# A router's mean taken in four groups of tiles, and the last output tiles in two pairs

## Reference

```python
xn = _layernorm(x)
x  = x + gnn(xn, edges) + mix(xn)              # x1: what the edge batches make
x2 = _layernorm(x)
logits = mean(x2, axis=nodes) @ Wr + br        # one row of 8
w = softmax(scale * softmax(logits)); top 2    # two experts, two weights
y = sum over the 2 experts: w_e * (gelu(x2 @ W1_e + b1_e) @ W2_e + b2_e)
x = x + layernorm(y + x2) * gamma + beta
```

## Time and profile before

| | us |
|---|---|
| median of 3 runs | 2583.76 (2582.44 to 2586.27) |
| the profiled execution | 2590.89 |
| its span | 2589.1 |
| busy: PE, DVE, ACT, POOL | 1962.0, 1677.4, 954.5, 1576.9 |
| mean granted TensorE clock in it | 0.867 of full speed |

### The profile page before, as it was taken

One profiled execution on the slowest core, in us unless ns is written; L12 is line 12 of the kernel. 1 busy time (PEld: TensorE's weight loads), 2 busy tenths in 40 slices (PEclk: granted clock), 3 DMA queues, 4 the chain that ended last, 5 costly groups with the idle time before them and its releaser, 6 DMA issues.

```text
span 2589.1 us, 32776 instructions
## 1 busy us (share of the span) xinstructions
PE 1962.0 (76%) x8612; PEld 1426.1 (55%) x8612; DVE 1677.4 (65%) x3588; ACT 954.5 (37%) x2092; POOL 1576.9 (61%) x1713
## 2 busy tenths in 40 slices
PE   5667787767776776867767678888787666899997
PEld 4545555545555554545555556666565443577775
DVE  6567676767767676666766677777778885333334
ACT  2533333333333343333333432323224554433332
POOL 2477777777777777777777777777777772000000
PEclk9878878888888888888888888888898778899998
DMA  7455555555555555555555556556555551100000
GB/s 234 153 157 147 148 146 147 149 147 147 148 148 146 148 146 145 153 140 148 148 145 146 141 158 172 163 165 167 165 163 144 135 138 40 39 19 18 18 18 20
DMA packets 171510, 337.61 MB, mean 130 GB/s; under 512 B 36500, under 2 KB 89466, under 8 KB 171342
## 3 DMA queue, kind: packets, MB, share of 16 engines
q0 software_dynamic: 78144, 220.11, 31.4%
q1 hardware_dynamic: 91854, 115.32, 15.4%
q10 hardware_dynamic: 1344, 0.27, 0.1%
HBM read 309.16 MB, written 26.39 MB: 130 GB/s over the span
## 4 chain that ended last, share of the span: by engine, by line
POOL 33%; PE 20%; issue 20%; DVE 11%; DMA 8%; POOLq 4%; ACT 3%; DVEq 2%; ACTq 0%; SPq 0%
POOL work L662 33%; DMA work<-h_tab,cols 7%; PE bank L1146 6%; PE bank L1136 5%; POOLq L655 4%; PE bank L1085 3%; DVE work L1535 3%; PE bank L921 1%; DVE zs L1476 1%; DVE acc L1543 1%; PE bank L1107 1%; DVE a2c L1478 1%; ACT work L756 1%; DVE a2c L1481 1%; DVE a2c L1480 1%
## 5 line engine op out<-in xcount | busy, mean ns | idle before, releaser
L662 POOL DMA_INDIRECT work<-h_tab,cols x1612 | 1531.4, 950 | 506.2 <-issue 466.2
L1085 PE MATMUL bank<-work 128*128 128x264 f32 x3608 | 1080.7, 455 | 33.4 <-DVE work L1535 33.4
L1085 PEld LDWEIGHTS bank<-work 128*128 128x128 f32 x3608 | 791.0, 226 | 212.9 <-DVE work L1535 37.9
L1535 DVE TENSOR_TENSOR work<-work,bank 128x1024 f32<-128x1024 f32 x451 | 547.9, 1215 | 116.3 <-issue 102.7
L762 ACT ACTIVATE bank<-a2c 128x64 f32<-128x64 f32 x226 | 51.5, 228 | 1230.2 <-DVE a2c L1483 1230.2
L978 PE MATMUL bank<-a2p,work 128*128 x1808 | 95.5, 195 | 436.0 <-ACT work L756 423.9
L978 PEld LDWEIGHTS bank<-a2p,work 128*128 128x128 bf16 x1808 | 77.1, 103 | 524.8 <-issue 518.1
L1476 DVE TENSOR_REDUCE zs<-bank 128x128 f32<-128x384 f32 x226 | 125.1, 554 | 370.6 <-POOLq L651 368.0
L1375 DVE TENSOR_TENSOR work<-bank,cols 128x1024 f32<-128x1024 f32 x226 | 275.0, 1217 | 0.0
L756 ACT ACTIVATE work<-work,ones 128x1024 bf16<-128x1024 bf16 x227 | 260.6, 1148 | 7.4
L754 ACT ACTIVATE work<-work,pcol 128x1024 bf16<-128x1024 bf16 x227 | 257.1, 1133 | 13.1 <-DMA work<-dst_d 13.1
(11 more groups left out here) (274 smaller groups left out, 1932.8 us busy)
## 6 DMA issues: line engine op xcount, KB each, us to landing
work<-dst_d SPq DMA_DIRECT2D x228, 256.0 KB, 3.9
work<-h_tab,cols POOLq DMA_INDIRECT x1612
xnt_c<-xnt_d SPq DMA_DIRECT2D x66, 128.0 KB
h_tab<-acc SPq DMA_DIRECT2D x49, 132.0 KB, 1.9
xnt_d<-acc SPq DMA_DIRECT2D x49, 128.0 KB, 2.1
q2t_d<-q2t_c SPq DMA_DIRECT2D x49, 128.0 KB, 2.2
out<-wqkv SPq DMA_DIRECT2D x16, 384.0 KB, 2.5
X<-x SPq DMA_DIRECT2D x5, 1024.0 KB, 11.2
```

The costliest lines, as they stand in the source:

```text
L662: nc.gpsimd.indirect_dma_start(out=work[:, (r * G + g) * TW:(r * G + g + 1) * TW], out_offset=None, in_=h_tab, in_offset=bass.IndirectOffs ...
L1085: ins = mm(bank[MB[n % len(MB)]][:, 0:TW], hot[b % HQ][:, s * G + g, :], M[n % MS][:, g, :], start=(g == 0), stop=(g == G - 1))
L1535: v.tensor_tensor(m, a, ex, ALU.mult).then_inc(msg_ready, 1)
```

## The change

The mean's tiles stand in four groups: 0 to 31, 32 to 41, 42 to 45, 46 to 48. The first group's variances are made in batch 219, its scale in batch 220, and its 32 matmuls run in batches 221 to 224, four behind each step. The second group's variances are made in batch 224 and its scale in batch 225, the others behind the batches. The row moves from bank 2 to bank 7, `nmr` to another place. On ScalarE only nine tiles instead of 18 are normalised, in the gaps of the router's chain, and Gelu's table is loaded before the choice is waited for; a `transposed` and a load for a batch that doesn't exist are left out. TensorE's wait for b2 and the scaled W2 moves behind `hidden(1)`. The last root of the pipeline stands behind `hidden(16)` and not inside it. Tiles 45 to 48 get b2 added to x2 and beta added to X beforehand and are finished in two pairs; the last pair is stored by two queues, a tile each.

```diff
-XG = [(0, 44), (44, NT)]
-XD = 18
+XG = [(0, 32), (32, 42), (42, 46), (46, NT)]
+VAR_AT = [219, 224]
+MEAN_AT = 221
+MEAN = 4
+XD = 9
...
-        nmr = zs[:].rearrange("p j a -> p (j a)")[:, 0:NT]
+        nmr = a2c[:, R3 * 3 * TB * H:R3 * 3 * TB * H + NT]
... SP
-                if not (isinstance(i, int) and i == IT):
+                if b + R3 < NB:
                     sp.wait_ge(a2c_picked, b + 1)
                     load_dst(b + R3, q)
...
+            store(NG - 2, 0)
+            t = NT - 4
+            sp.wait_ge(y_ready, NG)
+            sp.dma_start(out[t * P:(t + 2) * P, :].rearrange("(t p) c -> p t c", p=P), y[1][:, 0:2, :]).then_inc(out_stored[1], 16)
+            sp.wait_ge(y_ready, NG + 1)
+            sp.dma_start(out[(t + 2) * P:(t + 3) * P, :], y[0][:, 0, :]).then_inc(out_stored[0], 16)
... GpSimd
-            pool.wait_ge(x2_ready, 2 * FG)
-            stage(0, 0, FG)
-            stage(1, 1, FG)
+            for g in range(2):
+                pool.wait_ge(x2_ready, (g + 1) * FG)
+                stage(g, g, FG)
... ScalarE, in batch
+                if b + 2 < NB:
                     transposed(b + 2, (q + 2) % R3, i + 1 if q < 1 else i + 2)
+                if b == VAR_AT[1]:
+                    root(len(LN) + 1, rstd[:, XG[1][0]:XG[1][1]])
                 for t in range(*finished(b - 1)):
                     sums(t)
+                if b == VAR_AT[0]:
+                    root(len(LN), rstd[:, XG[0][0]:XG[0][1]])
+                    nc.scalar.activation(small[0:1, 30:31], small[0:1, 31:32], ACT.Exp)
... ScalarE, behind the batches
-            root(x2_root, rstd[:, XG[0][0]:XG[0][1]])
-            for t in range(*finished(NB - 1)):
+            sums(XG[3][0])
+            root(x2_root + 2, rstd[:, XG[2][0]:XG[2][1]])
+            for t in range(XG[3][0] + 1, NT):
                 sums(t)
-            sums(NT - 1)
-            root(x2_root + 1, rstd[:, XG[1][0]:XG[1][1]])
+            root(x2_root + 3, rstd[:, XG[3][0]:XG[3][1]])
             nc.scalar.activation(small[0:1, 30:31], small[0:1, 31:32], ACT.Exp)
-            act.wait_ge(x2_scaled, 1)
-            normal(0, 2 * FG)
             act.wait_ge(mean_made, 1)
-            nc.scalar.copy(sq[0:1, :], bank[2][0:1, 0:C]).then_inc(mean_kept, 1)
+            nc.scalar.copy(sq[0:1, :], bank[7][0:1, 0:C]).then_inc(mean_kept, 1)
             act.wait_ge(mean_made, 2)
             nc.scalar.copy(mcol[:], bank[1][:, 16:16 + KC]).then_inc(mean_kept, 1)
+            normal(0, 2)
             act.wait_ge(soft_in, 1)
             nc.scalar.activation(route[:, 2, :], route[:, 1, :], ACT.Exp).then_inc(soft_out, 1)
+            normal(2, 5)
             act.wait_ge(soft_in, 2)
             nc.scalar.activation(route[:, 6, :], route[:, 5, :], ACT.Exp).then_inc(soft_out, 1)
+            normal(5, XD)
             act.wait_ge(soft_in, 3)
             nc.scalar.activation(route[:, 12, 0:1], route[:, 11, 0:1], ACT.Exp).then_inc(soft_out, 1)
+            nc.scalar.activation(small[0:1, 30:31], small[0:1, 31:32], ACT.Gelu)
             act.wait_ge(chosen, 1)
...
-            normal(2 * FG, XD)
-            nc.scalar.activation(small[0:1, 30:31], small[0:1, 31:32], ACT.Gelu)
...
-            hidden(NG, 0, 1)
-            root(NG + len(LN) + len(XG) - 1, ysc[:, 1, 5, :])
-            root(NG + len(LN) + len(XG), ysc[:, 0, 5, 0:1])
+            hidden(NG, 0, 1, False)
+            root(NG + len(LN) + len(XG) - 2, ysc[:, 0, 5, :])
+            root(NG + len(LN) + len(XG) - 1, ysc[:, 1, 5, 0:2])
+            root(NG + len(LN) + len(XG), ysc[:, 0, 5, 0:2])
+            act.wait_ge(y_ready, NG + 1)
+            act.dma_start(out[(NT - 1) * P:N, :], y[0][0:LAST, 1, :]).then_inc(out_stored[0], 16)
... TensorE
+            row = bank[7][0:1, 0:C]
+            def mean_part(a, e):
+                for t in range(a, e):
+                    n = LAST if t == NT - 1 else P
+                    mm(row, rstd[0:n, t:t + 1], X[0:n, t, :], start=(t == 0), stop=False, skip_group_check=True)
...
                     between(i, q, side, first, s)
+                    if MEAN_AT <= b < NB - 1:
+                        pe.wait_ge(x2_scaled, 1)
+                        t = ((b - MEAN_AT) * SB + s) * MEAN
+                        mean_part(t, t + MEAN)
...
-            for g, (a, e) in enumerate(XG):
+            for g in range(1, len(XG)):
                 pe.wait_ge(x2_scaled, g + 1)
-                (the matmuls of the group)
+                mean_part(*XG[g])
...
-            pe.wait_ge(b2_ready, 1)
-            mm(bank[6][:, 0:C], ones[0:1, :], b2r[0:1, 2, :], start=True, stop=True).then_inc(b2_made, 1)
-            pe.wait_ge(w2_scaled, 1)
             for g in range(2):
                 hidden(g + 1, 1 - g, FG)
                 x2_in(g + 2, g, FG)
+                if g == 0:
+                    (the three lines above)
                 down(g, g, FG)
... VectorE, in batch
                 if last:
-                    x2_var(0)
+                    x2_scale(1)
...
-                if last:
+                if b in VAR_AT:
+                    x2_var(VAR_AT.index(b))
+                if b == VAR_AT[0] + 1:
                     x2_scale(0)
... VectorE, behind the batches
+            x2_var(2)
             dve.wait_ge(added, STEPS)
             divide(NT - 1, NT)
             plus(NT - 1, NT)
-            x2_var(1)
-            x2_scale(1)
+            x2_scale(2)
+            x2_var(3)
+            x2_scale(3)
... VectorE, the end
-            finish(NG, 0, 1)
+            t0 = NT - 4
+            dve.wait_ge(x2_staged, NG + 1)
+            a4 = acc[:, t0 * TW:NT * TW].rearrange("p (t w) -> p t w", w=TW)[:, :, 0:C]
+            v.tensor_tensor(a4, a4, b2w.unsqueeze(1).to_broadcast([P, 4, C]), ALU.add)
+            own(v.tensor_tensor(X[:, t0:NT, :], X[:, t0:NT, :], gb[:, 1, :].unsqueeze(1).to_broadcast([P, 4, C]), ALU.add))
+            finish(NG - 2, 0, FG)
+            def pair(k, p, stores):
+                t = t0 + 2 * k
+                dve.wait_ge(out_stored[p], 16 * stores)
+                yy = y[p][:, 0:2, :]
+                for j in range(2):
+                    dve.wait_ge(y_made, t + j + 1)
+                    v.tensor_tensor(y[p][:, j, :], bank[4 + (t + j - t0) % FG][:, 0:C], a4[:, t + j - t0, :], ALU.add).then_inc(y_added, 1)
+                (statistics, root, scaling of both tiles)
+                own(v.tensor_tensor(yy, yy, gb[:, 0, :].unsqueeze(1).to_broadcast([P, 2, C]), ALU.mult))
+                v.tensor_tensor(yy, yy, X[:, t:t + 2, :], ALU.add).then_inc(y_ready, 1)
+            pair(0, 1, NG // 2 - 1)
+            pair(1, 0, NG // 2)
```

More of the change, by code:

```diff
@@ L95 @@
 assert MS == len(MB) and KS == 512
+assert all(SB * (VAR_AT[g] - 2) - U + 1 == XG[g][1] for g in range(2)) and VAR_AT[1] == NB - 2
+assert SB * (NB - 2) - U + 1 == XG[2][1] and MEAN_AT > VAR_AT[0] + 1 and MEAN * SB * (NB - 1 - MEAN_AT) == XG[0][1]
 def wait(eng, sem, count):
@@ L541, in _ @@
             for q in range(R3):
-                sp.wait_ge(dst_in[q], 16 * (IT + 1))
+                sp.wait_ge(dst_in[q], 16 * ((NB - 1 - q) // R3 + 1))
             sp.wait_ge(added, STEPS)
-            sp.wait_ge(hotT_ready, NB + 1)
+            sp.wait_ge(hotT_ready, NB)
             sp.dma_start(gb[:, 0, :], gamma.unsqueeze(0).to_broadcast([P, C])).then_inc(e_loaded, 16)
@@ L561, in store @@
                 sp.wait_ge(y_ready, g + 1)
-                if isinstance(g, int) and g == NG:
-                    sp.dma_start(out[g * FG * P:N, :], y[p][0:LAST, 0, :]).then_inc(out_stored[p], 16)
-                    return
                 sp.dma_start(out[bass.ds(g * FG * P, FG * P), :].rearrange("(t p) c -> p t c", p=P),
                              y[p][:, :, :]).then_inc(out_stored[p], 16)
-            with sp.Fori(0, NG // 2) as i:
+            with sp.Fori(0, NG // 2 - 1) as i:
                 store(i * 2, 0)
                 store(i * 2 + 1, 1)
-            store(NG, 0)
-            sp.wait_ge(out_stored[0], 16 * (NG // 2 + 1))
+            store(NG - 2, 0)
[4 more added lines that the diff above has]
+            sp.dma_start(out[(t + 2) * P:(t + 3) * P, :], y[0][:, 0, :]).then_inc(out_stored[0], 16)
+            sp.wait_ge(out_stored[0], 16 * (NG // 2 + 2))
             sp.wait_ge(out_stored[1], 16 * (NG // 2))
@@ L1099, in x2_in @@
                 ins.then_inc(x2_turned, 1)
-            row = bank[2][0:1, 0:C]
-            for g, (a, e) in enumerate(XG):
+            for g in range(1, len(XG)):
                 pe.wait_ge(x2_scaled, g + 1)
-                for t in range(a, e):
-                    n = LAST if t == NT - 1 else P
-                    mm(row, rstd[0:n, t:t + 1], X[0:n, t, :], start=(t == 0), stop=False, skip_group_check=True)
+                mean_part(*XG[g])
             pe.wait_ge(rm_summed, 1)
@@ L1156, in _ @@
                 x2_in(g + 2, g, FG)
+                if g == 0:
+                    pe.wait_ge(b2_ready, 1)
```

(21 more changed lines are left out.)

## The result

The changed kernel takes 2555.69 us (median of 4 runs, 2554.76 to 2556.62), the one before 2583.55 (4 runs, 2582.44 to 2586.27): ratio 0.9892, interval 0.9878 to 0.9906, 27.9 us less. The profiled execution of the changed kernel took 2555.78 with a span of 2554.0.

A forecast was written before the change was run, and what follows sets the result against it. GpSimd's gather issue sets the pace during the edges, then a serial tail of 439 us follows. Terms -17.7 -5.8 +1.0 -8.3 make -30.8, -30.6 with displaced exponentials, off the median 2583.76: 2553.2 us, range 2546 to 2561.

The forecast's parts named there:

- The batches: Edge batches up to the last scale: added VectorE work delays them 0.4 us, bounds 0 and 1.2.
- The mean: Router's mean on TensorE: its end moves from 2192.5 to 2174.8, -17.7 us, bounds -18.1 and about -13.
- The rival of the lower clock: TensorE stays at 1.2 GHz through batches 221 to 225 and the mean: 2586, slower; 3 in 100, 5 for half.
- a half sentence: Edge batches on TensorE: more work per batch makes the higher clock level likelier; no size given.
- Router to first block: From the mean's end to hidden(0): it starts at 2205.8 instead of 2211.62 in the old time frame, -5.8 us.
- The rival "W1 lands late": First expert block waits for late W1, biases or W2 scaling: gains 2 instead of 5.8, 2557; 9 in 100.
- The wait for W2: Wait moved behind hidden(1) and x2_in(2), with nothing beside it: +1.0 us, bounds 0 and 1.3.
- The end: Last four tiles in pairs, root behind hidden(16): -8.4 us, less 0.1 for ScalarE's store issue, so -8.3.
- Table loads: ScalarE in batch 219: each load takes 1.28 us without the skill's 1.38 drain; 3.0 us extra hidden in 4.43 idle.
- the 0.1 to 0.2 for the exponentials: ScalarE's gaps in the router's chain: normals displace the exponentials, giving 0.1 to 0.2 us back.
- an assumption: Profiled old execution's 7.1 us above the median lie outside the tail, so the gain comes off the median.

The follow-up runs named there:

- e1: The kernel before, run and profiled once more with no edit: 2582.07 us, ratio 0.9997.
- e5: The kernel before with the new end alone (pairs, root behind hidden(16), two last stores): 2576.13 us, ratio 0.9974 to before.
- e2: The changed kernel with the mean's first group of 32 matmuls moved behind the last batch, variances and roots left in the batches: 2568.55 us.
- e7: The changed kernel with each of the 32 mean matmuls in the batches followed by a second one into unused columns: 2564.52 us.
- e6: The changed kernel with b2's matmul issued before hidden(1), only the scaled-W2 wait behind x2_in(2): 2549.66 us, ratio 0.9877 to before.
- e9: The kernel before with the mean's four groups alone, on a slower chip with gather pauses: 3261.46 us, ratio 0.9962 to before.
- e3: The changed kernel with the old end (root inside hidden(16), full triple and single, one last store): 2560.90 us.
- e4: The changed kernel with ScalarE's old order (18 tiles normalised, twelve normals and the Gelu load behind the choice): 2562.40 us.
- e8: The changed kernel with both last stores issued by SP instead of one by ScalarE: 2554.32 us.
- e11: The changed kernel, unedited, on the slower chip with gather pauses: 3246.52 us, ratio 0.9921 to before.

## Why the prediction was right, step by step

Forecast 2553.2 (2546 to 2561), measured 2555.69. The terms:

- **The batches** (+0.4, bounds 0 and 1.2): from the last gather to the last `scale` 13.93 us instead of 13.34, +0.6 (the old way took 12.78 and 13.26 in e1 and e5). From batch 219 to 225 it is 54.00 instead of 54.09, because VectorE's last wait for a gathered unit, 0.85 us in the earlier trace rows, took the rest of the delay as the working said: it is gone from the changed kernel's trace. e2 has the same delay (13.73) without the matmuls, so it isn't theirs; what is left is VectorE's additional work. e7 shows where the matmuls would begin to cost.
- **The mean** (-17.7 with the 0.4 in it, -18.1 from the last scale): 29.04 to 10.59, -18.45; with the 0.6 it is -17.9. By e2, 64 records fewer are 14.2 of it (15.0 counted). The block starts 3.3 us behind the last `scale` and no longer 6.2, as it doesn't wait for the root: 2.9. The last 1.3 is clock: the old block took 23.00 where e2's took 21.67. I read those 23.00 as the price at the high level and took 0.235 a record from them, but the granted clock over the block was 0.93, and a record costs 0.22. The size of the term depends on the execution: the old block took 21.32 in e5 (granted clock over it 1.00) and 23.52 in e1 (0.90), with segments of 27.35 and 29.55. So the term is worth 17 to 19. The rival of the lower clock had it the wrong way round: the added work raised the granted clock in the batches from 0.79 (e2) to 0.95, as the working had guessed in a half sentence without a term for it.
- **Router to first block** (-5.8): 19.29 to 13.60, -5.7. Right by luck in part, since misses cancel: +0.9, -1.6 and +0.8. The chain to the third exponential grew by 0.9 (8.5 to 9.4 from the mean's row), of which 0.58 and 0.34 are VectorE waiting out GpSimd's copies; I had priced ScalarE's gaps and not looked at what the copies of the tiles, which now run beside the router, do to VectorE. On the other side I had added 1.5 us for the Gelu load and its operation ahead of the bias transfers. The transfers were issued during the load, and the next copy started 2.3 us behind the third exponential, as long as without a load before. So the copies ended 1.6 earlier than worked out (3.2 behind the exponential, not 4.8), and W1 took over as the bound (0.83 us). The rival "W1 lands late" thus acts, for under a us; over the eight profiles with this order `hidden(0)` comes 12.95 to 13.76 behind the row, 13.5 forecast.
- **The wait for W2** (+1.0, bounds 0 and 1.3): `hidden(1)` 0.33 sooner behind `x2_in(1)` (2.09 to 1.76), the down projection 1.44 later behind `x2_in(2)`: +1.1. e6 gets the 1.4 back.
- **The end** (-8.4, and +0.1 behind it): 31.08 to 22.47, -8.6, of which by e9 up to 1.4 are the clock that fell in the old pause. Behind it +0.7 instead of +0.1. That was the worst-sized term: two stores take longer to land than one, 0.5 of it, and ScalarE's queue adds 0.2.
- **Table loads.** 1.28 and the next operation at once, in batch 219, ahead of every root and ahead of Gelu; the whole extra was 3.0 us inside idleness of 4.1. The drain that the Trainium skill ("ScalarE: Activation LUTs", "What ACT_TABLE_LOAD costs") adds to each switch appears nowhere on ScalarE in these traces. Each load took 1.28, and the next operation started within 0.02 us unless it waited for another engine.

From the first scale of batch 219 on the sum is -31.4 by the two profiles, and from the last gather on, with the 0.6, it is -30.7, against -30.8 with the 0.1 to 0.2 for the exponentials not counted. That the profiled execution of before was 7 us above its median for reasons outside the edited part was an assumption; e1 shows it: 7.3 us in the gather phase.

What remains is that the medians differ by 27.9 and not by 31. The variants narrow this: when the difference of each to the changed kernel, by its segments from batch 219 on, is put back to its median, e2, e3 and e4 give 28.6, 27.5 and 27.4 against the kernel before on their chip, e6, e7 and e8 32.4, 31.5 and 28.8 (estimates). With the 27.9 the mean is 29.2. Ten profiles on chips without the pauses have a gather phase between 2034.2 and 2041.7 us for the same instructions, both ends of the range with the old as with the new end of the program in place, and the interval of the first comparison (24.3 to 31.5) holds the forecast. e5 speaks against a shift that any edit brings, and cannot exclude one of 2 or 3 us; e9 and e11 ran on the chip with the pauses and can't settle it. That stays open.

## What to carry to other kernels

Work that waits for the last piece of a reduction can usually be done for all earlier pieces inside the loop ahead, and what it may cost there is the idle time per pass of the engine that does it. Here some 4 us of 9 could be filled, as doubling the work showed, partly because the busier TensorE ran at the higher clock. Ask also what the clock does: a block's price, read behind a pause, holds records at the lower level. When one stall goes, price the other edits again beside it, since ScalarE's order was worth 5.7 us with the old mean and 7.1 with the new one. And before reading a difference of 3 us from two profiles, profile the old kernel twice and compare by segments.

## What was not expected of the hardware

- VectorE's `tensor_scalar` on 1 x 8 numbers took 0.74 and 0.56 instead of 0.16 and 0.22 us when a GpSimd copy of 128 x 768 had started before it, each until the copy's end. So in all eight profiles with the new order (0.74 or 0.75, and 0.55 or 0.56), and 0.16 and 0.22 in the six others, where the copies run earlier (e4 and e9 among them, which have the early mean). A `tensor_reduce` that started 0.1 us into the second copy kept its 0.15. The Trainium skill, "SBUF — State Buffer", "Who interferes with whom", says of the port pair that VectorE and GpSimd share that it is an exclusive lock, that `tensor_scalar` can need it and `tensor_reduce` on trn2 never does. The trace agrees, with 0.74 for the one and 0.15 for the other.
- ScalarE's queue issues a transfer while its engine loads a table: issue at 2180.39, load from 2179.70 to 2180.98.
- Adding 3.5 us of matmuls to a batch made the matmuls that were there faster: the granted clock over the last four batches was 0.95 with them and 0.79 without (e2), an edge step 2.05 us and not up to 3.89.
- One and the same program's gather phase of 1612 indirect transfers differed by 7.3 us between two executions (the first profile and e1), and on one chip it was 690 us longer, with pauses whose origin the records don't show.
